# Query times key-value state in linear attention: one 64-row matmul per head, numerator and normaliser side by side, in place of block-diagonal 128-row ones

## The chip, the cores and the metric

The kernel runs on one core of a Trainium2 chip. A core has a matrix engine (PE, with its weight loads shown as PEld), a vector engine (DVE), a scalar engine (ACT), a general-purpose engine (POOL, also called GpSimd) and a queue engine (SP) that here only starts transfers. PE writes its results to PSUM, eight banks of 128 partitions by 512 four-byte values; the other data lie in SBUF. The metric is the device time of one execution in microseconds (us), as the median over runs.

## The reference

Two layers, each a modulated layer norm followed by a mixer, then another followed by a feed-forward part, with residual additions. Only the first mixer, linear attention with 32 heads of 64, is touched by the change; x is 4 x 512 x 512.

```python
q = relu(proj(Wq)); k = relu(proj(Wk)); v = proj(Wv)          # [b, 32, 512, 64]
kv = einsum('bhsd,bhse->bhde', k, v)                          # the state, 64 x 64 a head
qkv = einsum('bhsd,bhde->bhse', q, kv)
key_sum = k.sum(axis=2)
normalizer = clip(einsum('bhsd,bhd->bhs', q, key_sum), 1e-06, None)[..., None]
out = qkv / normalizer
return out.transpose(0, 2, 1, 3).reshape(b, s, INNER) @ Wo + bo
```

The second feed-forward part keeps the two largest of each four hidden values (stage D below); the first one routes rows to two of eight experts (stage B).

## The kernel before, in words

All matmuls of note are done with 32-bit operands split into a high and a low part (HI, LO): a product is three matmuls, HI by HI, HI by LO, LO by HI, accumulated in one bank. The helper `mm3` issues the three; its lines are L670 to L672, so most matmuls of the kernel stand under these lines and are told apart by their tile names. The split of a result takes two engines: ACT copies the HI part out of PSUM, then DVE subtracts it from the full value to get the LO part.

There is one program for each engine, written by hand in order; nothing schedules them but semaphores. Stage A (attention) has 8 groups of 4 heads (g), and in each a step for each of the 4 batch entries (b): 32 steps, s = 4g + b. The groups 1 to 6 are one loop body. Later stages are B (experts), C and D (sparse feed-forward).

One step on PE: four key/value projections of 128 rows each (t = 0 to 3, 12 matmuls of 512 columns, into bank 0 or 1), after each of which but the first the state of the tile before is accumulated in bank 4 (`accumulate(t-1)`, 6 matmuls of 130 columns, tiles kt and vt); two query projections, with the last accumulation between them; the output projection of the step before (`tail_a`, "tail" below, 24 matmuls with ot and the weights wo in W1b); and last the product of queries and state (12 matmuls, tiles kvb and qt). The four heads of a group form two pairs; a pair fills the 128 partitions of qt. The stationary tile kvb holds for each pair a block-diagonal 128x128 matrix of the two states (kind 0) and one of the two key sums, each repeated 64 times (kind 1), with zeros elsewhere, set once at the start. Kind 1 goes first, into banks 5 and 4, kind 0 after it into banks 6 and 7.

What happens to the result: DVE clips both normalisers from PSUM into rr (L1725), inverts pair 0 at the end of the step (`invert`, L1653) and pair 1 in the next step behind the low parts of tile 0. In the next step, at t = 2 and 3, `normalise` (L1658) multiplies the numerator in PSUM by rr; then `out_hi` on ACT (L1131) and `out_lo` on DVE (L1663) split it into ot, which the tail reads. The low parts of keys and values are L1673 and L1675, those of queries L1702, those of the state L1713 and L1715, and the evacuation of the tail is L1647. PE's `accumulate(0)` waits for both clips of the step before (r_max).

POOL adds the tail's results to x (L1978) and makes the low parts of weights that ACT has copied from a stage buffer (L1048 on ACT, `wsplit`, L1916 on POOL, 1024 columns each). In groups 1 to 6 the steps b = 1 and 2 split expert weights (tile W) and b = 3 splits two slices of the next attention weights (W1a), all ahead of the output's HI part in ACT's order; one further slice of these weights (W1b) is split at the end of b = 3 and one at the end of b = 0.

## Time and profile before

| | before |
|---|---|
| time, median of 3 runs | 2059.91 us (2056.55 to 2063.98) |
| profiled execution | 2059.06 us, span 2057.1 us |
| PE busy | 1835.3 us (89%), 8300 matmuls |
| weight loads busy | 1461.9 us (71%) |
| DVE busy | 1271.7 us (62%), 2094 instructions |
| ACT busy | 548.8 us (27%) |
| POOL busy | 775.0 us (38%) |

The busy time of PE is the sum of modelled spans that overlap, so it says that PE is hardly ever without a matmul, not that it runs at its peak. Stage A runs from about 25 to 1010 us.

### The profile page before, as it was taken

Reading aid. Unit: us, or ns where it says so; the run is one execution under the profiler, and the core shown is the slowest. Engines: PE = TensorE matmul, PEld = TensorE weight load, DVE = VectorE, ACT = ScalarE, POOL = GpSimd, SP = SyncE. Lnnn points to the kernel's source line nnn. Section 1 sums busy time; section 2 is a strip of 40 time slices with the busy share of each in tenths; the row PEclk is TensorE's granted clock in tenths of the full one; section 3 lists DMA queues with packets and bytes.
Section 4 is the critical chain, followed back from the end, with each engine's and each line's share of the span. In section 5 each row is a group of like instructions: output and inputs, shape, how many; then the busy total and the mean of one; then the engine's idle time right before and its main releaser. Section 6 shows DMA issues by size and latency. Waiting matters only on the chain.

```text
span 2057.1 us, 25161 instructions
## 1 busy us (share of the span) xinstructions
PE 1835.3 (89%) x8300; PEld 1461.9 (71%) x8300; DVE 1271.7 (62%) x2094; ACT 548.8 (27%) x1120; POOL 775.0 (38%) x565
## 2 busy tenths in 40 slices
PE   8999999999999999998547999735689999999996
PEld 5657888888888888877445777324478778787785
DVE  5665666666666666677852323588957565657574
ACT  2322222223222222212113343323342222212221
POOL 1545433433333333221350000475744454536342
PEclk9999999999999999999758999967799999999998
DMA  6211444434243525200146764330200111001011
GB/s 225 98 67 64 144 164 143 163 126 161 80 179 112 194 74 206 87 21 16 62 179 225 293 245 159 121 109 16 62 26 10 48 29 49 10 25 51 6 52 41
DMA packets 75070, 213.01 MB, mean 104 GB/s; under 512 B 6588, under 2 KB 6604, under 8 KB 72432
## 3 DMA queue, kind: packets, MB, share of 16 engines
q1 hardware_dynamic: 57072, 149.00, 20.5%
q0 software_dynamic: 6592, 42.04, 5.6%
q10 hardware_dynamic: 11328, 20.98, 3.4%
q8 instruction: 44, 0.72, 0.1%
q14 instruction: 34, 0.28, 0.0%
HBM read 126.20 MB, written 85.79 MB: 103 GB/s over the span
## 4 chain that ended last, share of the span: by engine, by line
PE 60%; DVE 21%; issue 9%; DMA 4%; POOL 3%; ACT 2%; DVEq 0%; ACTq 0%; POOLq 0%; SPq 0%
PE bank L670 19%; PE bank L672 18%; PE bank L671 18%; DMA hs_d<-yt 3%; DVE hh L1896 2%; PE bank L736 2%; DVE rr L1653 1%; POOL W1a L1916 1%; DVE st L1400 1%; POOL x L1978 1%; DVE tmp L1647 1%; DVE fl L1874 1%; DVE rstd L1384 1%; PE bank L701 1%; DVE xw L1452 1%
## 5 line engine op out<-in xcount | busy, mean ns | idle before, releaser
L1978 POOL TENSOR_TENSOR x<-x,tmp 128x512 f32<-128x512 f32 x192 | 264.8, 1389 | 484.3 <-DVE tmp L1647 431.3
L670 PE MATMUL bank<-hT,W1b 128*128 128x512 f32 x512 | 208.3, 407 | 11.4 <-DVE hh L1851 11.2
L1653 DVE RECIPROCAL rr<-rr 128x512 f32<-128x512 f32 x64 | 213.8, 3342 | 0.0
L670 PE MATMUL bank<-W1a,hT 128*128 128x512 f32 x512 | 206.9, 404 | 3.4 <-DVE hT L1579 3.4
L672 PE MATMUL bank<-W1a,hT 128*128 128x512 f32 x512 | 202.7, 396 | 0.0
L672 PE MATMUL bank<-hT,W1b 128*128 128x512 f32 x512 | 202.2, 395 | 0.0
L671 PE MATMUL bank<-hT,W1b 128*128 128x512 f32 x512 | 202.1, 395 | 0.0
L671 PE MATMUL bank<-W1a,hT 128*128 128x512 f32 x512 | 202.0, 394 | 0.0
L1144 ACT ACTIVATE kt<-bank 128x256 fp32r<-128x256 f32 x128 | 49.1, 384 | 551.4 <-PE bank L672 551.4
L1647 DVE TENSOR_TENSOR tmp<-bank,row 128x512 f32<-128x512 f32 x176 | 121.2, 689 | 78.3 <-PE bank L672 53.9
L1851 DVE TENSOR_TENSOR hh<-hh,bank 128x512 f32<-128x512 f32 x64 | 43.3, 687 | 184.9 <-PE bank L672 156.8
L1673 DVE SCALAR_TENSOR_TENSOR kt<-bank,kt 128x256 fp32r<-128x256 f32 x128 | 52.2, 408 | 147.4 <-ACT vt L1145 147.1
L1916 POOL TENSOR_TENSOR W<-stage,W 128x1024 fp32r<-128x1024 f32 x32 | 76.7, 2397 | 165.3 <-ACT W L1048 163.0
L670 PEld LDWEIGHTS bank<-hT,W1b 128*128 128x128 f32 x512 | 97.5, 190 | 35.5 <-DVE hh L1851 16.2
L670 PE MATMUL bank<-W1b,ot 128*128 128x512 f32 x256 | 105.8, 413 | 17.7 <-DVE tmp L1644 12.7
L670 PEld LDWEIGHTS bank<-W1a,hT 128*128 128x128 f32 x512 | 97.7, 191 | 27.7 <-issue 4.7
L672 PEld LDWEIGHTS bank<-hT,W1b 128*128 128x128 f32 x512 | 97.5, 190 | 22.2
L672 PEld LDWEIGHTS bank<-W1a,hT 128*128 128x128 f32 x512 | 97.4, 190 | 22.0
L670 PE MATMUL bank<-W,ad 128*128 128x512 f32 x256 | 101.6, 397 | 10.9 <-DVE ad L1903 9.1
L671 PEld LDWEIGHTS bank<-W1a,hT 128*128 128x128 f32 x512 | 97.8, 191 | 18.8
L671 PEld LDWEIGHTS bank<-hT,W1b 128*128 128x128 f32 x512 | 97.9, 191 | 18.5
L1345 ACT ACTIVATE ad<-hh 128x512 fp32r<-128x512 f32 x64 | 40.3, 632 | 252.7 <-DVE hh L1896 252.7
(258 smaller groups left out, 4424.0 us busy)
## 6 DMA issues: line engine op xcount, KB each, us to landing
hs_d<-bor SPq DMA_DIRECT2D x24, 1536.0 KB, 9.1
WB<-ws_d POOLq DMA_DIRECT2D x8, 3072.0 KB
ws_d<-W SPq DMA_DIRECT2D x18, 1024.0 KB, 6.4
stage<-wa SPq DMA_DIRECT2D x32, 512.0 KB, 5.1
row<-mod_rows_d ACTq DMA_DIRECT2D x52, 256.0 KB, 3.3
stage<-wbe SPq DMA_DIRECT2D x24, 512.0 KB, 3.9
stage<-wdn SPq DMA_DIRECT2D x24, 512.0 KB, 3.9
mw<-wmod SPq DMA_DIRECT2D x10, 1024.0 KB, 4.9
```

The costliest lines, as they stand in the source:

```text
L670: pe.matmul(o, lhs(HI), rhs(HI), start=start, stop=False, **kw)
L671: pe.matmul(o, lhs(HI), rhs(LO), start=False, stop=False, **kw)
L672: return pe.matmul(o, lhs(LO), rhs(HI), start=False, stop=stop, **kw)
L736: last = pe.matmul(o[0:NB, :], scT[:, layer, c, :], w[:, c * H:(c + 1) * H], start=c == 0, stop=c == NC - 1)
L1144: act.activation(kt[:, t % 2, HI, :], bank[t % 2][:, 0:256], ACT.Relu)
L1647: dve.tensor_tensor(tmp[:, par, :], TAIL[par][:, :], row[:, tb % 2, :], ALU.mult) \
L1653: dve.reciprocal(rr[:, pair, :], rr[:, pair, :]).then_inc(r_rec, 1)
L1673: dve.scalar_tensor_tensor(out=kt[:, t % 2, LO, :], in0=bank[t % 2][:, 0:256], scalar=0.0, in1=kt[:, t % 2, HI, :].bitcast(F32), op0=ALU.m ...
L1851: dve.tensor_tensor(hh[:, r, :], hh[:, r, :], bank[4 + r % 2][:, :], ALU.mult).then_inc(d_h, 1)
L1896: op(dve.scalar_tensor_tensor(out=hh[:, r, :], in0=flag, scalar=bound, in1=hh[:, r, :], op0=cmp, op1=ALU.mult))
L1916: return pool.tensor_tensor(dst, src, hi.bitcast(F32), ALU.subtract)
L1978: pool.tensor_tensor(xt, xt, tmp[:, (key + t) % 2, :], ALU.add).then_inc(ring_done, 1)
```

## The change

Each head gets a 64-row matmul of its own. Pair by pair, kvb now holds for partitions 0 to 63 the state of head 0 in columns 0 to 63 and its repeated key sum in columns 64 to 127; for partitions 64 to 127 it is the other way round. So there are no zeros in it, and it has half the size. A matmul with partitions 0 to 63 of kvb and qt writes numerators to the upper 64 partitions and normalisers to the lower 64 of one bank ("top"), one with partitions 64 to 127 the reverse in another ("low"): banks 5 and 6 for pair 0, 7 and 4 for pair 1. The matmuls of the two heads alternate. The count per step stays at 12.

The two numerators of a pair then lie in two banks. ACT gathers them in the new SBUF tile num (`num_out`, two copies of 64 partitions per pair), which shares its memory with the LO half of ot. The clip is written as two instructions of 64 partitions per pair, each shifting the normalisers to the other partition half. `normalise`, `out_hi` and `out_lo` work on num instead of PSUM. nn_full now counts two per step instead of four, and the new semaphore n_out counts ACT's copies; PE's first accumulation waits for it.

```diff
@@ -304,8 +304,12 @@
             return (a("kt", [P, 2, 2, 256], F32R), a("vt", [P, 2, 2, 2, VW], F32R), a("qt", [P, 2, 2, S], F32R),
-                    a("ot", [P, 2, 2, S], F32R), a("kvb", [P, 2, 2, 2, P], F32R), a("rr", [P, 2, S]),
+                    a("ot", [P, 2, 2, S], F32R), a("kvb", [P, 2, 2, P], F32R), a("rr", [P, 2, S]),
                     a("bor", [P, H]), a("colrow", [NB, H]))
+
+        def over_ot(a):
+
+            return a("before_num", [P, 5136]), a("num", [P, 2, S])
@@ -318,8 +322,8 @@
-        ((_, wm), (kt, vt, qt, ot, kvb, rr, bor, colrow), h2, (M_, crow, sqj, ct, cs),
-         (hh, mx, fl, ad)) = shared([over_pro, over_a, over_front, over_c, over_d])
+        ((_, wm), (kt, vt, qt, ot, kvb, rr, bor, colrow), (_, num), h2, (M_, crow, sqj, ct, cs),
+         (hh, mx, fl, ad)) = shared([over_pro, over_a, over_ot, over_front, over_c, over_d])
         hold3 = sb("hold3", [P, 9232])
@@ -373,6 +377,7 @@
         TAIL = bank[2:4]
+        NN = [(5, 6), (7, 4)]
         YB = [0, 1, 4, 5, 6, 7]
@@ -810,6 +816,7 @@
                         pe.wait_ge(r_max, s * 2)
+                        pe.wait_ge(n_out, s * 2)
                     for pair in range(2):
@@ -852,10 +859,13 @@
                 pe.wait_ge(kvb_lo, s + 1)
-                for kind, banks in ((1, (5, 4)), (0, (6, 7))):
-                    for pair in range(2):
-                        mm3(bank[banks[pair]][:, :], lambda h: kvb[:, h, pair, kind, :],
-                            lambda h: qt[:, h, pair, :], True, True).then_inc(nn_full, 1)
+                for pair in range(2):
+                    for i, (wl, wr) in enumerate(((HI, HI), (HI, LO), (LO, HI))):
+                        for head in range(2):
+                            q = slice(head * HD, (head + 1) * HD)
+                            last = pe.matmul(bank[NN[pair][head]][:, :], kvb[q, wl, pair, :], qt[q, wr, pair, :],
+                                             start=i == 0, stop=i == 2)
+                    last.then_inc(nn_full, 1)
@@ -931,8 +941,8 @@
                 pe.wait_ge(r_max, 2 * NB * GA)
+                pe.wait_ge(n_out, 2 * NB * GA)
                 pe.wait_ge(pj_lo, 6 * NB * GA)
-                pe.wait_ge(o_lo, 2 * NB * GA)
                 rows_transpose(0)
@@ -1128,7 +1138,14 @@
                 act.wait_ge(o_num, s * 2 + (pair - 1))
-                act.activation(ot[:, HI, pair, :], bank[6 + pair][:, :], ACT.Copy).then_inc(o_hi, 1)
+                act.activation(ot[:, HI, pair, :], num[:, pair, :], ACT.Copy).then_inc(o_hi, 1)
+
+            def num_out(s, pair):
+
+                act.wait_ge(nn_full, s * 2 + (pair + 1))
+                top, low = (bank[i] for i in NN[pair])
+                act.activation(num[0:HD, pair, :], top[0:HD, :], ACT.Copy)
+                act.activation(num[HD:P, pair, :], low[HD:P, :], ACT.Copy).then_inc(n_out, 1)
@@ -1172,7 +1189,7 @@
                     if pair == 0 and not (first and b == 0):
-                        act.wait_ge(nn_full, s * 4)
+                        act.wait_ge(nn_full, s * 2)
                     act.activation(qt[:, HI, pair, :], bank[pair][:, :], ACT.Relu).then_inc(pj_hi, 1)
@@ -1183,9 +1200,9 @@
                 for lo in (0, HD):
-                    q = slice(lo, lo + HD)
-                    act.activation(kvb[q, HI, :, 0, q], kv[q, :, q], ACT.Copy)
-                    ins = act.activation(kvb[q, HI, :, 1, q], kv[q, :, P:P + 1].to_broadcast([HD, 2, HD]), ACT.Copy)
+                    q, other = slice(lo, lo + HD), slice(HD - lo, P - lo)
+                    act.activation(kvb[q, HI, :, q], kv[q, :, q], ACT.Copy)
+                    ins = act.activation(kvb[q, HI, :, other], kv[q, :, P:P + 1].to_broadcast([HD, 2, HD]), ACT.Copy)
                 ins.then_inc(kvb_hi, 1)
@@ -1194,6 +1211,8 @@
                     split_a(g, 3)
+                for pair in range(2):
+                    num_out(s, pair)
@@ -1558,7 +1577,6 @@
                 dve.memset(bor[:, :], 0.0).then_inc(zero_ready, 1)
-                dve.memset(kvb[:, :, :, :, :].bitcast(F32), 0.0)
                 dve.memset(vt[:, :, HI, :, P:VW].bitcast(F32), 1.0)
@@ -1653,15 +1671,14 @@
             def normalise(s, pair):
-                dve.wait_ge(nn_full, s * 4 + (pair - 1))
+                dve.wait_ge(n_out, s * 2 + (pair - 1))
                 dve.wait_ge(r_rec, s * 2 + (pair - 1))
-                dve.tensor_tensor(bank[6 + pair][:, :], bank[6 + pair][:, :], rr[:, pair, :], ALU.mult) \
-                    .then_inc(o_num, 1)
+                dve.tensor_tensor(num[:, pair, :], num[:, pair, :], rr[:, pair, :], ALU.mult).then_inc(o_num, 1)
...
                 dve.wait_ge(o_hi, s * 2 + (pair - 1))
-                dve.tensor_tensor(ot[:, LO, pair, :], bank[6 + pair][:, :],
-                                  ot[:, HI, pair, :].bitcast(F32), ALU.subtract).then_inc(o_lo, 1)
+                dve.tensor_tensor(ot[:, LO, pair, :], num[:, pair, :], ot[:, HI, pair, :].bitcast(F32),
+                                  ALU.subtract).then_inc(o_lo, 1)
@@ -1709,21 +1726,21 @@
                 for lo in (0, HD):
-                    q = slice(lo, lo + HD)
-                    dve.tensor_tensor(kvb[q, LO, :, 0, q], kv[q, :, q], kvb[q, HI, :, 0, q].bitcast(F32),
-                                      ALU.subtract)
-                    last = dve.tensor_tensor(kvb[q, LO, :, 1, q], kv[q, :, P:P + 1].to_broadcast([HD, 2, HD]),
-                                             kvb[q, HI, :, 1, q].bitcast(F32), ALU.subtract)
+                    q, other = slice(lo, lo + HD), slice(HD - lo, P - lo)
+                    dve.tensor_tensor(kvb[q, LO, :, q], kv[q, :, q], kvb[q, HI, :, q].bitcast(F32), ALU.subtract)
+                    last = dve.tensor_tensor(kvb[q, LO, :, other], kv[q, :, P:P + 1].to_broadcast([HD, 2, HD]),
+                                             kvb[q, HI, :, other].bitcast(F32), ALU.subtract)
                 last.then_inc(kvb_lo, 1)
...
                 for pair in range(2):
-                    dve.wait_ge(nn_full, s * 4 + (pair + 1))
+                    dve.wait_ge(nn_full, s * 2 + (pair + 1))
                     if tail_of("A", g, b):
                         dve.wait_ge(o_num, s * 2)
-                    dve.tensor_scalar(rr[:, pair, :], bank[(5, 4)[pair]][:, :], 1e-6, None, ALU.max) \
-                        .then_inc(r_max, 1)
+                    top, low = (bank[i] for i in NN[pair])
+                    dve.tensor_scalar(rr[0:HD, pair, :], top[HD:P, :], 1e-6, None, ALU.max)
+                    dve.tensor_scalar(rr[HD:P, pair, :], low[0:HD, :], 1e-6, None, ALU.max).then_inc(r_max, 1)
                 invert(s + 1, 0)
```

On PE the place is the end of a step in the first group, the last matmuls of the tail (W1b, ot) and the product (qt, kvb). Before:

```order
L670 MATMUL bank<-W1b,ot 128x512
L671 MATMUL bank<-W1b,ot 128x512
L672 MATMUL bank<-W1b,ot 128x512
L670 MATMUL bank<-qt,kvb 128x512 [waits a_kvb_lo,a_proj_lo]
L671 MATMUL bank<-qt,kvb 128x512
L672 MATMUL bank<-qt,kvb 128x512
L670 MATMUL bank<-qt,kvb 128x512
L671 MATMUL bank<-qt,kvb 128x512
```

After:

```order
L676 MATMUL bank<-W1b,ot 128x512
L677 MATMUL bank<-W1b,ot 128x512
L678 MATMUL bank<-W1b,ot 128x512
L866 MATMUL bank<-qt,kvb 128x512 [waits a_kvb_lo,a_proj_lo]
L866 MATMUL bank<-qt,kvb 128x512 x11
L676 MATMUL bank<-W1a,hT 128x512 [waits a_proj_lo,ring_done]
L677 MATMUL bank<-W1a,hT 128x512
```

There are still twelve matmuls, now all under one line (L866), between the same neighbours; what moved is which rows and banks they use, and the waits ahead of them are the same.

On DVE the first place is the end of a step in the loop body, from the last evacuation of the tail (tmp) through the clips (rr) to the next step's first low parts (kt, vt). Before:

```order
L1647 TENSOR_TENSOR tmp<-bank,row 128x512 [waits ring_done,ring_full]
L1722 REGISTER_ALU
L1725 TENSOR_SCALAR rr<-bank 128x512 [waits a_out_normalised,a_norm_num_full]
L1722 REGISTER_ALU
L1725 TENSOR_SCALAR rr<-bank 128x512 [waits a_out_normalised,a_norm_num_full]
L1652 ISA
L1653 RECIPROCAL rr<-rr 128x512 [waits a_norm_clipped]
L1672 ISA
L1673 SCALAR_TENSOR_TENSOR kt<-bank,kt 128x256 [waits a_proj_hi]
L1675 TENSOR_TENSOR vt<-bank,vt 128x2x128
L1653 RECIPROCAL rr<-rr 128x512 [waits a_norm_clipped]
```

After:

```order
L1665 TENSOR_TENSOR tmp<-bank,row 128x512 [waits ring_done,ring_full]
L1738 REGISTER_ALU
L1742 TENSOR_SCALAR rr<-bank 64x512 [waits a_out_normalised,a_norm_num_full]
L1743 TENSOR_SCALAR rr<-bank 64x512
L1738 REGISTER_ALU
L1742 TENSOR_SCALAR rr<-bank 64x512 [waits a_out_normalised,a_norm_num_full]
L1743 TENSOR_SCALAR rr<-bank 64x512
L1670 ISA
L1671 RECIPROCAL rr<-rr 128x512 [waits a_norm_clipped]
L1689 ISA
L1690 SCALAR_TENSOR_TENSOR kt<-bank,kt 128x256 [waits a_proj_hi]
L1692 TENSOR_TENSOR vt<-bank,vt 128x2x128
```

Two clips have become four, of 64 partitions each, ahead of the same reciprocal.

The second place on DVE is the middle of the step: normalising, the low parts of the output and those of the queries (the last t in the loop body). Before:

```order
L1658 TENSOR_TENSOR bank<-bank,rr 128x512 [waits a_norm_inverted,a_norm_num_full]
L1672 REGISTER_ALU
L1673 SCALAR_TENSOR_TENSOR kt<-bank,kt 128x256 [waits a_proj_hi]
L1675 TENSOR_TENSOR vt<-bank,vt 128x2x128
L1658 TENSOR_TENSOR bank<-bank,rr 128x512 [waits a_norm_inverted,a_norm_num_full]
L1663 TENSOR_TENSOR ot<-bank,ot 128x512 [waits a_out_hi] x2
L1701 REGISTER_ALU
L1702 SCALAR_TENSOR_TENSOR qt<-bank,qt 128x512 [waits a_proj_hi]
L1701 REGISTER_ALU
L1702 SCALAR_TENSOR_TENSOR qt<-bank,qt 128x512 [waits a_proj_hi]
```

After:

```order
L1676 TENSOR_TENSOR num<-num,rr 128x512 [waits a_norm_inverted,a_num_copied]
L1689 REGISTER_ALU
L1690 SCALAR_TENSOR_TENSOR kt<-bank,kt 128x256 [waits a_proj_hi]
L1692 TENSOR_TENSOR vt<-bank,vt 128x2x128
L1676 TENSOR_TENSOR num<-num,rr 128x512 [waits a_norm_inverted,a_num_copied]
L1680 TENSOR_TENSOR ot<-num,ot 128x512 [waits a_out_hi] x2
L1718 REGISTER_ALU
L1719 SCALAR_TENSOR_TENSOR qt<-bank,qt 128x512 [waits a_proj_hi]
L1718 REGISTER_ALU
L1719 SCALAR_TENSOR_TENSOR qt<-bank,qt 128x512 [waits a_proj_hi]
```

Number and order are the same; the operand bank has become num in the three instructions of normalising and of the output's low part.

## Rows read from the trace of the kernel before

**Rows 1.** Windows: length, busy us of PE, PEld, DVE, ACT, POOL, clock, DMA, GB/s.
```profile
274.00:388.00 114.00, 113.68 (x545) 94.13 (x544) 74.00 (x108) 30.50 (x74) 39.56 (x24) 1.00 0.39 138
```

**Rows 2.** Timeline of PE, one step: start us, us, engine, line, operation.
```profile
486.26 0.39 PE L670 MATMUL bank<-qt,kvb 128*128 128x512 f32 x1
...
489.02 0.39 PE L670 MATMUL bank<-W1a,hT 128*128 128x512 f32 x1
...
494.48 0.22 PE L670 MATMUL bank<-vt,kt 128*128 128x130 f32 x1
...
497.92 0.22 PE L670 MATMUL bank<-vt,kt 128*128 128x130 f32 x1
...
508.23 0.40 PE L670 MATMUL bank<-W1b,ot 128*128 128x512 f32 x1
...
513.83 0.39 PE L670 MATMUL bank<-qt,kvb 128*128 128x512 f32 x1
```

**Rows 3.** Timeline of DVE, the same step.
```profile
487.15 1.38 DVE L1725 TENSOR_SCALAR rr<-bank 128x512 f32<-128x512 f32 x2
488.45 3.34 DVE L1653 RECIPROCAL rr<-rr 128x512 f32<-128x512 f32 x1
492.73 0.42 DVE L1673 SCALAR_TENSOR_TENSOR kt<-bank,kt 128x256 fp32r<-128x256 f32 x1 [0.94 <-ACT vt L1145]
...
496.94 0.41 DVE L1675 TENSOR_TENSOR vt<-bank,vt 128x256 fp32r<-128x256 f32 x1
...
503.00 0.69 DVE L1658 TENSOR_TENSOR bank<-bank,rr 128x512 f32<-128x512 f32 x1
504.70 1.29 DVE L1663 TENSOR_TENSOR ot<-bank,ot 128x512 fp32r<-128x512 f32 x2 [1.01 <-ACT ot L1131]
```

**Rows 4.** Timeline of PE, group 0, where 4-row transposes begin.
```profile
149.36 0.39 PE L672 MATMUL bank<-W1a,hT 128*128 128x512 f32 x1
149.68 0.41 PE L743 MATMUL bank<-ident,colrow 4*128 4x4 f32 x4
```

**Rows 5.** Groups by line and shape, attention stage: xcount, busy us, mean ns.
```profile
L1713 DVE TENSOR_TENSOR kvb<-bank,kvb 64x128 fp32r<-64x128 f32 x46 | 13.0, 284 | 0.3
```

**Rows 6.** Timeline of DVE and PE after the next product (T = 513.83).
```profile
517.36 1.28 DVE L1725 TENSOR_SCALAR rr<-bank 128x512 f32<-128x512 f32 x2
518.55 3.34 DVE L1653 RECIPROCAL rr<-rr 128x512 f32<-128x512 f32 x1
...
522.64 0.32 PE L670 MATMUL bank<-vt,kt 128*128 128x130 f32 x1 [0.43 <-DVE vt L1675]
```

**Rows 7.** Line L1663 (ns min/median/max), then timeline, stages D and C.
```profile
L1663 DVE TENSOR_TENSOR ot<-bank,ot x64: 669/682/692, 82.5 to 1009.0; 128x512 fp32r<-128x512 f32 x64
...
1606.05 2.41 POOL L1916 TENSOR_TENSOR W1b<-stage,W1b 128x1024 fp32r<-128x1024 f32 x1 [2.10 <-ACT W1b L1048]
1606.11 2.89 DVE L1870 TENSOR_TENSOR mx<-xn 128x512 f32<-128x512 f32 x1
...
1422.67 6.36 DVE L1452 TENSOR_TENSOR xw<-xw,crow 128x512 f32<-128x512 f32 x4
```

**Rows 8.** Timeline of POOL in the step of rows 2; line L1916, 209 to 850.
```profile
503.40 4.95 POOL L1916 TENSOR_TENSOR W1a<-stage,W1a 128x1024 fp32r<-128x1024 f32 x2 [14.87 <-ACT W1a L1048]
...
L1916 POOL TENSOR_TENSOR W<-stage,W x24: 2392/2408/2412, 226.0 to 811.7; 128x1024 fp32r<-128x1024 f32 x24
L1916 POOL TENSOR_TENSOR W1a<-stage,W1a x12: 2400/2404/2408, 281.3 to 839.3; 128x1024 fp32r<-128x1024 f32 x12
```

**Rows 9.** Groups by line and shape of ACT, attention stage.
```profile
L1131 ACT ACTIVATE ot<-bank 128x512 fp32r<-128x512 f32 x46 | 25.6, 603 | 4.7 <-DVE bank L1658 4.7
```

**Rows 10.** Timeline of PE in group 7 and after; windows view around the first.
```profile
916.35 0.48 PE L670 MATMUL bank<-vt,kt 128*128 128x130 f32 x1 [3.24 <-DVE vt L1675]
912.00:919.00 7.00, 3.76 (x14) 3.01 (x14) 5.72 (x29) 0.66 (x2) 0.00 (x0) 0.79 0.00 0
...
1009.69 0.80 PE L670 MATMUL bank<-W1b,ot 128*128 128x512 f32 x1 [4.95 <-DVE ot L1663]
```

More of the change, by code:

```diff
@@ L420, in build @@
         nn_full = sem("a_norm_num_full")
+        n_out = sem("a_num_copied")
         r_max = sem("a_norm_clipped")
@@ L1433, in apply_rows @@
                 if b >= 2:
-                    dve.wait_ge(nn_full, 4 * NB * GA)
+                    dve.wait_ge(nn_full, 2 * NB * GA)
                 for t in range(NT):
```

## Prediction

> **What bounds the kernel now.** The page comes first: PE is the busiest engine over the whole span. The windows view says where: in 114 us of attention in steady state PE is busy for 113.68, the vector engine DVE for 74.00 [rows 1]. A shorter PE stage looks like pure gain, so the question is what ends next when it is shorter. For that I followed one step of the attention stage in the timeline, engine by engine. T is the start of its first query-times-state matmul; in [rows 2] T = 486.26. The twelve matmuls take 489.02 - 486.26 = 2.76 us (0.23 each, start to start; a row says 0.39 because recorded spans overlap). Two key/value projections follow, then the first accumulation at T+8.22, a third projection, the second accumulation at T+11.66, then the output projection ("tail") at T+21.97, and the next product at T+27.57.
>
> DVE in the same step [rows 3]: it clips two normalisers from T+0.89, runs a reciprocal of 3.34, takes the low parts of tile 0's keys and values from T+6.47 after 0.94 idle for ACT, runs the second reciprocal, and has the low part of tile 1's values at T+10.68+0.41 = T+11.09. The second accumulation needs that, at T+11.66. So this chain has 0.57 us of slack against PE, and 0.94 of idleness inside. That is what a faster product meets, not the 40 idle microseconds of DVE in rows 1.
>
> **The product on PE.** It stays at 12 matmuls a step in 32 steps, each 512 columns, now with 64 rows. Nothing in this trace has 64 rows. Lower bound: two heads' matmuls, in separate row halves and banks, run side by side: 6 x 0.23 = 1.39. Upper bound: one after another, 2.76. A change of the rows in use costs too: ahead of the 4-row transposes the gap between starts is 0.32 instead of 0.23 [rows 4], 0.09 more. Leaving such a shape isn't shown alone; for entering and leaving I take 0.35, between 0.18 (0.09 twice) and 0.78 (two whole matmul records of 0.39). I take side by side, 1.39 + 0.35 = 1.74: 1.0 us saved a step, 32 us in all if PE alone decided. One after another it would lose 0.35 a step, 11 us. No row decides between them.
> The Trainium skill (TensorE: Matmul & The Clock Gate, Part 3: Packing small matmuls — row/col tiling) says that matmuls in different row groups overlap; by that rule the product takes the side-by-side time. The Trainium skill (TensorEngine Tiling (Array Packing), Key Properties) also says that a change of tiling mode drains the engine; the wider gap in rows 4 agrees.
>
> **The clipping on DVE.** One 128x512 instruction per pair becomes two of 64x512, because each head's bank holds the normaliser in its other half. Does half the height cost half? The 64x128 subtraction takes 0.28 [rows 5], a 128x256 one 0.41 and a 128x512 one 0.69 [rows 3]: these lie on one line in the elements of a row, 0.14 plus 0.27 for each 256, whatever the height. So each half costs a full one; at 1.19 for two, start to start [rows 6], a step gets +1.2. (If height counted, 0: the other bound.) The first can start when pair 0 is done, about T+1.1 (0.69 of matmuls, 0.2 for the switch, 0.2 to finish). The new chain: four clips to T+3.5, reciprocal to 6.75, keys and values to 7.4 (ACT has them an estimated 1.0 earlier than before, so nothing is waited for), reciprocal to 10.7, tile 1's values at T+11.3. The second accumulation starts at T+11.45, where PE could have been by T+10.6. Of the 1.0 saved, 0.2 is left in an ordinary step.
>
> **Late steps.** After the product of the fourth batch entry (T = 513.83) output additions on POOL hold up the last evacuations, and DVE clips only from T+3.53; PE already waits 0.43 for values [rows 6]. Here +1.2 goes straight to the end, and PE's saving does not help. I take 1.2 in group 0 and 0.6 in each of groups 1 to 6, since POOL's last split ends sooner relative to T once the step before is longer (next part): 4.8 us.
>
> **Normalising and the output's low part, now in SBUF.** These four DVE instructions a step keep number and size, but both inputs lie in SBUF; before, one was in PSUM. With one PSUM input 64 low parts took 0.669 to 0.692, none longer [rows 7], although POOL splits weights right beside them: two splits, 4.95 us from T+17.14 [rows 8], the low parts from T+18.44 [rows 3]. Now instructions with two SBUF inputs: in the sparse stage one began at 1606.11, beside a split from 1606.05 to 1608.46, and took 2.89 to 1609.00: it waited for the split's end. Four in a row beside POOL's work took 6.36, 1.59 each: the engines take turns [rows 7]. Put into the step: POOL's first split runs 17.2 to 19.6, once the second normalising is over. The first low part is asked for at 18.25, waits, runs 19.6 to 20.2. POOL's second split goes 20.25 to 22.65. The second low part runs 22.65 to 23.25, and the tail starts at T+23.31 in place of T+21.97: +1.34 a step. (Bounds: with no wait at all -0.2; behind both splits about the same 1.3.) Such pairs of splits stand in 18 steps of groups 1 to 6: 24 + 12 instructions [rows 8], two a step. 18 x 1.34 = 24.1 us, and one such step in group 0, 1.2.
> The Trainium skill (SBUF — State Buffer, Who interferes with whom) has this as a rule: a DVE instruction with two SBUF inputs and a GpSimd one that reads SBUF exclude each other, and the first to issue wins. It speaks against this change, and the trace agrees (2.89 for 0.69).
>
> **The rest.** ACT gets four copies of 64x512 a step, 0.6 each by its 128x512 copy [rows 9], done by about T+3.5; PE asks for them at the first accumulation, T+7. ACT is idle until the first projection ends. That cover of 3.5 us is what hides them; without it they would cost what they lack. In group 0 three steps leave DVE time, and PE's saving shows in two: -2. In group 7 one step gains 0.2; the one where PE waits 3.24 for DVE gets +1.2; two later ones an estimated 0.6 each; after the last step PE waits 4.95 for the output's low part, +1.2 [rows 10]. Together +3.4. The clearing of kvb that goes away stands before the first input has arrived: 0. Outside attention nothing changes.
>
> **Sum.** 24.1 + 1.2 + 4.8 + 3.4 - 2 = +31.5. The profiled execution took 2059.06 (span 2057.10, 1.96 around it), 0.85 below the median of 2059.91. 2059.06 + 31.5 = 2090.6; I say 2090.
>
> **Rivals.**
> 1. *Serial halves.* For it: no 64-row matmul in the trace, so nothing shows that two run at once. The product then takes 3.1; pair 1 is clipped only from T+3.1, the chain ends at T+12.2, 0.85 later than in my case, in about 24 steps: +20, 2110.
> 2. *No turn-taking at the low part.* DVE gets both its turns after the first split and is done at T+20.9, before the tail's need. Against it: 1.59 each for four in a row [rows 7]. Then 31.5 less 19 x 1.4 is +5: 2064.
> 3. *PE's saving shows (faster).* The place is the clip: if 64 rows cost about half of 128, the chain ends at T+10.2 and PE is the bound at both accumulations. It decides only if the low parts also slip past the splits; then 32 x 1.0 less: 2027, and 2043 with half of it. Against it: rows 5 with rows 3.
> 4. *The clock.* Around the 3.24 wait the granted clock averages 0.79 over 7 us [rows 10]: 2.9 us at the lower level (1.2 GHz), some 1.5 us lost. If a wait of 1.3 before each tail did this too, 19 x 1.5 = 28 more: 2118. Against it: the 0.43 wait stands in a stage at 1.00 [rows 1, 6]; no row here has one of 1.3.
>
> **Numbers.** Forecast 0.50 (2080 to 2100), serial 0.20, no turns 0.13, faster 0.09, clock 0.08. Less than 0.3% (6 us) can't be told from no change in this kernel. Faster than that 0.08, within it 0.10, slower 0.82. Range 2064 to 2114: it takes in serial and most of no turns, and leaves out the clock and the gain.
>
> **What would show it.** Right: 1.7 us from the first 64-row matmul to the next projection; 64x512 clips of 0.69; low parts of up to 2.9 us in 18 steps and PE idle before the tail there; PE waiting for tile 1's values in most steps. Wrong: low parts at 0.69 throughout; 64-row matmuls 0.23 apart one by one; clips at 0.4; no wait at the second accumulation.

## The result, and the profile after

| | before | changed |
|---|---|---|
| time, median of 4 runs each | 2061.94 us (2056.55 to 2064.02) | 2097.03 us (2095.99 to 2099.69) |
| profiled execution | 2059.06, span 2057.1 | 2096.59, span 2094.6 |
| product of the fourth entry of the last group starts | 998.26 | 1029.01 |

The changed kernel is slower, by a ratio of 1.0176 (interval 1.0152 to 1.0200), about 35 us. The last row of the table shows that 31 of them have come by the end of attention's steps (T of the last product). I use that moment below wherever a run can be compared by attention alone; the later stages are the same code and move by a few us from run to run. A *late step* is one that begins with the product of the fourth batch entry; the *ordinary steps* are the other 18 of groups 1 to 6.

The page of the profile after, the engines' busy time and the chain that ended last:

```profile
PE 1821.1 (87%) x8300; PEld 1421.6 (68%) x8300; DVE 1374.1 (66%) x2157; ACT 626.5 (30%) x1248; POOL 782.0 (37%) x565
...
PE 49%; DVE 26%; issue 12%; DMA 4%; ACT 4%; POOL 4%; ACTq 0%; DVEq 0%; POOLq 0%; SPq 0%
```

PE has less to do and the time is longer: its busy time fell by 14 us, DVE's rose by 102. About four steps by windows, from the same groups as [rows 1] (the columns are those of [rows 1]):

```profile
284.00:401.00 117.00, 109.79 (x527) 86.53 (x526) 87.62 (x112) 38.95 (x88) 40.21 (x25) 0.99 0.38 134
```

PE stands idle for 7.2 us of the 117 where it stood idle for 0.3 of 114. An ordinary step, beginning with the product at T = 703.26, shows both places. PE (timeline: start, busy, line, tiles, and in brackets the idle time ahead and what ended it):

```profile
702.93 0.40 PE L678 MATMUL bank<-W1b,ot 128*128 128x512 f32 x1
703.26 1.66 PE L866 MATMUL bank<-qt,kvb 64*128 64x512 f32 x12
704.85 0.50 PE L676 MATMUL bank<-W1a,hT 128*128 128x512 f32 x1
705.18 0.40 PE L677 MATMUL bank<-W1a,hT 128*128 128x512 f32 x1
...
711.31 0.30 PE L676 MATMUL bank<-vt,kt 128*128 128x130 f32 x1 [0.71 <-DVE vt L1692]
...
714.99 0.33 PE L676 MATMUL bank<-vt,kt 128*128 128x130 f32 x1
...
726.60 0.50 PE L676 MATMUL bank<-W1b,ot 128*128 128x512 f32 x1 [1.03 <-DVE ot L1680]
```

The product takes 1.59 us from its first matmul to the next projection, where [rows 2] show 2.76. At each change of rows two starts are 0.33 behind their neighbour and not 0.23. One of the two lies outside the product at either end (702.93 to 703.26, 704.85 to 705.18), so the net gain is 2.76 - 1.59 - 0.2 = 0.97 us. It is then waited away: 0.71 at the first accumulation, for the low part of the values, and 1.03 ahead of the tail, for the output's low part. The tail now starts at T+23.34 (T+21.97 before, [rows 2]). The same step on DVE:

```profile
704.27 0.69 DVE L1742 TENSOR_SCALAR rr<-bank 64x512 f32<-64x512 f32 x1 [0.21 <-PE bank L866]
704.97 0.68 DVE L1743 TENSOR_SCALAR rr<-bank 64x512 f32<-64x512 f32 x1
705.69 0.69 DVE L1742 TENSOR_SCALAR rr<-bank 64x512 f32<-64x512 f32 x1
706.39 0.68 DVE L1743 TENSOR_SCALAR rr<-bank 64x512 f32<-64x512 f32 x1
707.11 3.35 DVE L1671 RECIPROCAL rr<-rr 128x512 f32<-128x512 f32 x1
710.38 0.36 DVE L1690 SCALAR_TENSOR_TENSOR kt<-bank,kt 128x256 fp32r<-128x256 f32 x1
710.66 0.41 DVE L1692 TENSOR_TENSOR vt<-bank,vt 128x256 fp32r<-128x256 f32 x1
...
720.17 0.68 DVE L1676 TENSOR_TENSOR num<-num,rr 128x512 f32<-128x512 f32 x1
721.91 4.56 DVE L1680 TENSOR_TENSOR ot<-num,ot 128x512 fp32r<-128x512 f32 x2 [1.06 <-ACT ot L1141]
```

DVE goes from the first clip to the values without a gap; before, it had 0.94 to spare there [rows 3]. And the two low parts, 1.29 for both in [rows 3], take 4.56. What runs beside them is POOL's pair of splits, 4.95 before [rows 8]:

```profile
720.49 5.43 POOL L1933 TENSOR_TENSOR W<-stage,W 128x1024 fp32r<-128x1024 f32 x2 [15.06 <-ACT W L1058]
```

Over all 64 low parts (view of one line's instructions: minimum, median, maximum in ns), and how long PE waited for them (us, times):

```profile
L1680 DVE TENSOR_TENSOR ot<-num,ot x64: 670/1750/2892, 82.0 to 1041.3; 128x512 fp32r<-128x512 f32 x64
...
  PE bank L676: 26.8, 19
```

From product to product an ordinary step takes 29.11 to 29.23 us, 27.55 to 27.57 before: +1.6 on the mean, 28.7 in all 18.

### The profile page after: what moved, and what is told of

Its sections match the earlier page's. It is cut to its first block, busy times and chain, and to the rows that moved or that the text cites. A ratio compares the mean times of both kernels' runs of the same rounds, so it can differ in the third digit from the quotient of the medians.

```text
span 2094.6 us, 25406 instructions
## 1 busy us (share of the span) xinstructions
PE 1821.1 (87%) x8300; PEld 1421.6 (68%) x8300; DVE 1374.1 (66%) x2157; ACT 626.5 (30%) x1248; POOL 782.0 (37%) x565
## 4 chain that ended last, share of the span: by engine, by line
PE 49%; DVE 26%; issue 12%; DMA 4%; ACT 4%; POOL 4%; ACTq 0%; DVEq 0%; POOLq 0%; SPq 0%
PE bank L676 15%; PE bank L678 14%; PE bank L677 14%; DMA hs_d<-yt 3%; DVE rr L1671 3%; DVE hh L1913 2%; DVE ot L1680 2%; PE bank L742 2%; DVE rr L1743 2%; POOL W1a L1933 1%; DVE st L1419 1%; ACT W L1058 1%; PE bank L866 1%; DVE tmp L1665 1%; POOL x L1995 1%
## 5 line engine op out<-in xcount | busy, mean ns | idle before, releaser
L1933 POOL TENSOR_TENSOR W<-stage,W 128x1024 fp32r<-128x1024 f32 x32 | 82.5, 2577 | 168.6 <-ACT W L1058 166.3
L676 PEld LDWEIGHTS bank<-W1a,hT 128*128 128x128 f32 x512 | 97.7, 191 | 37.3 <-issue 13.8
L1680 DVE TENSOR_TENSOR ot<-num,ot 128x512 fp32r<-128x512 f32 x64 | 104.3, 1657 | 21.2 <-ACT ot L1141 20.1
L678 PEld LDWEIGHTS bank<-W1a,hT 128*128 128x128 f32 x512 | 97.5, 190 | 22.1
```

Of the source, the lines that this page charges most:

```text
L676: pe.matmul(o, lhs(HI), rhs(HI), start=start, stop=False, **kw)
L678: return pe.matmul(o, lhs(LO), rhs(HI), start=False, stop=stop, **kw)
L1680: dve.tensor_tensor(ot[:, LO, pair, :], num[:, pair, :], ot[:, HI, pair, :].bitcast(F32), ALU.subtract).then_inc(o_lo, 1)
L1933: return pool.tensor_tensor(dst, src, hi.bitcast(F32), ALU.subtract)
```

## The experiments

All were run on one chip per set, with the kernel before at 2060 to 2061 us in each set; ratios are to it. "Last product" is the moment of the table above. Cut lines of a diff are marked "...".

### 1. Both splits behind the low parts

In steps b = 1 to 3 POOL waits until the output's low parts are made, and splits then.

```diff
-                if b == 3 and not (isinstance(g, int) and g == GA - 1):
+                last = isinstance(g, int) and g == GA - 1
+                if b > 0 and not (last or (first and b < 3)):
+                    pool.wait_ge(o_lo, (g * NB + b) * 2)
+                if b == 3 and not last:
                     for j in range(2 if first else 3):
                         split_a(g + 1, j)
...
```

> The changed kernel, and POOL waits for the output's low parts before its weight splits (steps b = 1 to 3). Turn-taking theory (a low part with two SBUF inputs waits for a split on POOL): low parts go back to 0.67 us each, the 1.0 us wait of PE before the output projection goes, step of 29.1 becomes 27.9; 18 x 1.2 = 22 us less, but the later splits can push POOL's additions and the clips of the step after b = 3, up to 6 back: 2075 to 2081. Rival (PE waits there for ACT or for a slower SBUF read, whatever POOL does): low parts stay long, 2097.

Measured: 2114.03 us (2110.12 to 2116.51), ratio 1.0263 (1.0246 to 1.0280). The low parts are back to 1.29 for both, there is no wait ahead of the tail, and the ordinary steps take 27.80 to 27.85: 1.3 less, as the turn-taking explanation says. But the six late steps of groups 1 to 6 go from 28.7 to 30.2 up to 34.2 to 35.8. I had looked at the place where the wait helps, not at what follows it on POOL (timeline of POOL around one product at T = 291.39):

```profile
283.74 4.95 POOL L1933 TENSOR_TENSOR W1a<-stage,W1a 128x1024 fp32r<-128x1024 f32 x2 [17.89 <-DVE ot L1680]
291.92 2.40 POOL L1933 TENSOR_TENSOR W1b<-stage,W1b 128x1024 fp32r<-128x1024 f32 x1 [3.22 <-ACT W1b L1058]
294.27 5.01 POOL L1995 TENSOR_TENSOR x<-x,tmp 128x512 f32<-128x512 f32 x4
```

The third split and the additions come late, the evacuations wait for the additions, the clips wait for the evacuations, and start at T+6.25 (T+2.00 in the changed kernel). PE then waits 5.5 to 6.1 us for values in each of the six, and the clock falls: its mean over the step of T = 646.79 is 0.86. The upper end of the forecast, 2081, was missed by 33 us.

### 2. Reciprocals behind the low parts of keys and values

Both reciprocals are taken out of the way of the tiles that PE waits for: pair 0 after tile 0's low parts, pair 1 after tile 1's.

```diff
-                        if t == 0:
-                            invert(s, 1)
+                        if t < 2:
+                            invert(s, t)
...
-                invert(s + 1, 0)
```

> The changed kernel with each of the two reciprocals one tile later (pair 0 behind tile 0's low parts, pair 1 behind tile 1's), all else the same. Theory (the chain clip, clip, clip, clip, reciprocal, low parts, reciprocal, low parts is what ate PE's gain): both accumulations wait no more, the second starts at 10.6 instead of 11.7 us after the product; about 1.1 less in 19 steps and 1.5 to 2 less in 7 late ones: 2097 - 21 - 12 = 2064. The 1.0 wait before the output projection stays. Rival (PE's gain is eaten by something else, such as waiting for ACT's evacuation): less than 8 us gained.

Measured: 2064.61 us (2058.75 to 2069.85), ratio 1.0020 (1.0008 to 1.0031), last product 996.99. Nothing but DVE's order is changed, and 32 us come back. In groups 1 to 6 the first accumulation starts at T+7.16 and the second at T+10.60, neither with a wait; ordinary steps take 27.9 to 28.0, late ones 26.6. The wait of 1.01 ahead of the tail stays, with low parts of 4.55 for both. In group 0 two steps became longer (41.56 and 48.84, from 37.95 and 44.49): in the first of them PE now waits 2.97 for values at the third accumulation. In the late steps of groups 1 to 6 the clips still start as late as T+2.2 and the step has no wait: late clips cost their time there through the order of DVE, and by themselves cost nothing.

### 3. The kernel before with four clips

```diff
-                    dve.tensor_scalar(rr[:, pair, :], bank[(5, 4)[pair]][:, :], 1e-6, None, ALU.max)
+                    dve.tensor_scalar(rr[0:HD, pair, :], o[0:HD, :], 1e-6, None, ALU.max)
+                    dve.tensor_scalar(rr[HD:P, pair, :], o[HD:P, :], 1e-6, None, ALU.max)
```

> The kernel before with only the clips changed: each of the two 128x512 clips a step written as two of 64x512 in the same bank. Theory (half the height costs a full instruction, 0.7 each here, +1.5 a step, hidden by slack in ordinary steps and open in late ones): clips at 0.69, ordinary steps unchanged within 0.1 (27.6), late ones +1.4 in 7 steps, after the last step +1.5, group 7 up to +1.5: +10 to +14, 2073. Rival (64 rows cost half): clips at 0.4, 2062.

Measured: 2084.01 us (2082.98 to 2087.18), ratio 1.0116 (1.0099 to 1.0133), last product 1017.19, 18.9 later. The clips of one step (timeline of DVE):

```profile
266.08 0.68 DVE L1726 TENSOR_SCALAR rr<-bank 64x512 f32<-64x512 f32 x1
266.78 0.69 DVE L1727 TENSOR_SCALAR rr<-bank 64x512 f32<-64x512 f32 x1
267.50 0.68 DVE L1726 TENSOR_SCALAR rr<-bank 64x512 f32<-64x512 f32 x1
268.20 0.69 DVE L1727 TENSOR_SCALAR rr<-bank 64x512 f32<-64x512 f32 x1
```

Half the height costs the full 0.69, and they start 0.70 to 0.72 apart, where two clips of 128 rows were 0.60 apart ([rows 6]). Here this splits within one bank and shifts nothing across the halves, and costs the same as in the changed kernel, so neither the shift nor the second bank is the reason. The ordinary steps hide nearly all of it (27.8, +0.24); the late ones of groups 1 to 6 do not (30.3 to 31.6, +1.8 to +3.3). The clips were forecast rightly, but the time missed the forecast of +10 to +14 by 10 us: a late step had been given only 1.4. In two of the six, and in the late step of group 0, the clock fell behind the wait (mean 0.94 over the step of T = 406.92, which takes 31.32, and 1.00 over that of T = 292.99, which takes 30.55).

### 4. The kernel before with the numerator in SBUF

The block-diagonal product stays; ACT copies the numerators to num, and normalising and the output's parts read them there.

```diff
...
+                act.activation(num[:, pair, :], bank[6 + pair][:, :], ACT.Copy).then_inc(n_out, 1)
...
-                dve.tensor_tensor(ot[:, LO, pair, :], bank[6 + pair][:, :],
+                dve.tensor_tensor(ot[:, LO, pair, :], num[:, pair, :],
```

> The kernel before with its block-diagonal product and its banks, but ACT copies the two numerators (128x512 each) to num in SBUF, and normalising and the output's parts work there. Turn-taking theory: low parts of up to 2.9 us beside POOL's splits, PE waits 1.2 before the output projection in 18 steps, 18 x 1.4 = 25, less 3 for late steps: 2084. Rival (it is the 64-row product or its waits that costs, not SBUF inputs): 2062.

Measured: 2079.74 us (2077.17 to 2081.23), ratio 1.0095 (1.0078 to 1.0112), last product 1013.38, 15.1 later. The low parts take what they take in the changed kernel:

```profile
254.41 4.57 DVE L1673 TENSOR_TENSOR ot<-num,ot 128x512 fp32r<-128x512 f32 x2 [1.05 <-ACT ot L1136]
```

Ordinary steps 28.84 to 28.94 (+1.3), late ones 27.55 to 27.6 (-0.9, since POOL's third split then ends sooner relative to T). Experiments 3 and 4 move the last product by 18.9 and 15.1, 34.0 us in sum, and the whole change moves it by 30.8. If the two simply add, which no run shows, the side-by-side product gives back only some 3 us of its 32 x 0.97.

### 5. The three matmuls of a head in a row

```diff
-                    for i, (wl, wr) in enumerate(((HI, HI), (HI, LO), (LO, HI))):
-                        for head in range(2):
+                    for head in range(2):
+                        for i, (wl, wr) in enumerate(((HI, HI), (HI, LO), (LO, HI))):
```

> The changed kernel with only the order of the twelve 64-row matmuls altered: for each pair all three of head 0, then all three of head 1. If two neighbours run side by side only when they stand in different row halves (my theory: the matmuls are issued in order, and 1.59 us for twelve comes from the alternation), three of four neighbours share a half and follow each other 0.23 apart: the product takes 2.3 to 2.8 us in place of 1.59, the clips of pair 0 start about 0.4 later, the first and second accumulation are late by that, and the time is 2097 + 32 x 0.4 = 2110 (2104 to 2118). Rival: the halves have queues of their own and the order doesn't matter: product 1.59, time 2097.

Measured: 2097.85 us (2096.26 to 2099.10), ratio 1.0181 (1.0149 to 1.0214); product 1.59 or 1.60. My expectation was wrong and its rival right: alternating the halves one by one is not needed, runs of three overlap as well. PE, same place as above:

```profile
705.13 1.67 PE L866 MATMUL bank<-qt,kvb 64*128 64x512 f32 x12
706.72 0.50 PE L676 MATMUL bank<-W1a,hT 128*128 128x512 f32 x1
```

### 6. All twelve matmuls in one half

That left open whether two halves work at once or a 64-row matmul is simply cheaper. Here head 0 is computed twice and head 1 not at all:

```diff
-                            q = slice(head * HD, (head + 1) * HD)
+                            q = slice(0, HD)
```

> The changed kernel in which all twelve 64-row matmuls of a product use partitions 0 to 63 (head 0 is computed twice, head 1 not at all), so that no two of them can run side by side. Theory (two halves at once): they follow each other 0.23 apart, the product takes 2.8, the clips of pair 1 start at about T+1.6 and T+3.0, the four clips end at T+4.4 in place of 3.85 and PE has 0.6 to 1.2 less to wait: +0.3 to +1.0 a step, the last product about 10 to 30 us later than 1029. Rival (a 64-row matmul of 512 columns costs half of a 128-row one by itself): product 1.59, nothing changes. The values that follow differ, so the experts' stage may take another number of slots: the place of the last product and the product's length decide.

Measured: product 2.94 us, last product 1048.49 (19.5 later than in the changed kernel), 2133.54 us in all.

```profile
715.68 3.01 PE L866 MATMUL bank<-qt,kvb 64*128 64x512 f32 x12
718.62 0.50 PE L676 MATMUL bank<-W1a,hT 128*128 128x512 f32 x1
```

A 64-row matmul costs a full 0.23 from start to start (2.94 for twelve, with two changes of rows in it); the gain is that two halves work at once. The Trainium skill (TensorE: Matmul & The Clock Gate, Why this matters for your kernels) says both: a matmul of few rows takes as long as a full one, and the gain lies in running distinct row groups concurrently. The traces agree, with 2.94 for one half and 1.59 for two.

### 7. One turn for DVE between the two splits

Experiment 1 held both splits back. Here only the second waits, in the steps that split expert weights as shown and in those of b = 3 between the first two slices. In an ordinary step it starts at T+21.2 in place of T+20.0.

```diff
...
                     split_e(g, 2 * b - 2)
+                    pool.wait_ge(o_lo, (g * NB + b) * 2)
                     split_e(g, 2 * b - 1)
```

> The changed kernel with one wait on POOL: in the steps of b = 1, 2 and 3 the second of the two weight splits starts only when both low parts of the output are made, the first one stays where it is. Turn-taking theory: DVE gets both its turns after the first split (19.7 to 21.0 after T), the low parts are done 2.3 earlier, the tail starts at T+22.1 without a wait, and an ordinary step takes 27.9 in place of 29.13: 19 x -1.2 = -23; the second split starts only 0.7 later than now (20.9 in place of 20.2), unlike when both splits were held back, so the late steps gain at most 1 us each: +0 to +7. Time 2077 (2072 to 2084). Rival: any wait that binds POOL to DVE is passed on to POOL's additions and comes back in the late steps, as when both splits were held back: 2092 to 2110.

Measured: 2092.10 us (2088.54 to 2095.09), ratio 1.0154 (1.0118 to 1.0190), last product 1023.66. The low parts take 2.35 for both, no wait is left ahead of the tail (T+22.14), ordinary steps are 27.83: -1.3 each, as expected. But the late steps of groups 1 to 6 take 30.1 to 32.8. The number fits the rival; its mechanism does not. POOL's third split starts at T+25.57 of the step before, 25.40 in the changed kernel: the wait hardly delays it. What happened is that PE's step got 1.3 shorter and POOL's did not, so the clips start at T+3.45 (T+2.00 in the changed kernel) and PE waits 3.0 to 3.2 us for the values in each of the six. In four of them the clock then falls. Windows of the one at T = 295.47 (columns as above, the granted clock third from the end), and PE behind the wait:

```profile
302.00:304.00 2.00, 0.79 (x4) 0.33 (x2) 2.00 (x1) 0.66 (x2) 0.00 (x0) 1.00 0.00 0
304.00:306.00 2.00, 0.03 (x1) 0.06 (x1) 2.00 (x4) 0.00 (x0) 0.00 (x0) 0.77 0.00 0
306.00:308.00 2.00, 2.00 (x8) 1.90 (x9) 2.00 (x1) 0.00 (x0) 0.00 (x0) 0.50 0.00 0
308.00:310.00 2.00, 2.00 (x7) 1.52 (x6) 1.59 (x3) 0.00 (x0) 0.00 (x0) 0.50 0.00 0
310.00:312.00 2.00, 2.00 (x6) 1.58 (x5) 0.00 (x0) 0.00 (x0) 0.00 (x0) 0.53 0.00 0
312.00:314.00 2.00, 2.00 (x13) 1.77 (x12) 0.80 (x3) 0.66 (x2) 0.00 (x0) 1.00 0.00 0
```

```profile
305.97 0.45 PE L676 MATMUL bank<-vt,kt 128*128 128x130 f32 x1 [3.17 <-DVE vt L1692]
...
307.28 0.73 PE L676 MATMUL bank<-W1a,hT 128*128 128x512 f32 x1
...
312.24 0.22 PE L676 MATMUL bank<-vt,kt 128*128 128x130 f32 x1
```

Six accumulations take 1.31 us and twelve projections 4.96, 6.27 together, where an ordinary step has 3.68 from the first accumulation to the second. So the wait of 3.17 is followed by another 2.5 us lost at 1.2 GHz: this step of 32.76 is 27.83, 2.45 for the later first accumulation, and 2.5 for the clock. The two late steps whose clock stays at 1.00 take 30.12 and 30.27: 27.83 and 2.3 to 2.4, with nothing else.

### 8. The same, with POOL's additions ahead of the third split

The test of that reading: take the late clips away, leave all else.

```diff
-                    if not first:
-                        split_a(g + 1, 2)
...
                 if not first:
                     ln_out(ln, 1)
+                if b == 3 and not (first or last):
+                    split_a(g + 1, 2)
```

> The kernel with only the wait between POOL's two splits (2092), and the third split of b = 3 (W1b) moved behind POOL's additions; the reciprocals stay where the changed kernel has them. Theory: what held its late steps at 31.5 was one wait of 3.2 us, which the later clips caused, and the half clock that followed. With the additions first the clips start at T+1, the wait is 0.7 as in an ordinary step, the clock stays at 1.00 and a late step of groups 1 to 6 takes 27.85 in place of 31.5 to 32.8: -4 x 6 = -24, 2068 (2062 to 2073). Rival: the half clock comes from something else in the late step and stays: 2085 to 2092.

Measured: 2064.93 us (2059.42 to 2070.07), ratio 1.0022 (1.0009 to 1.0034), last product 1001.14. In the late steps of groups 1 to 6 the clips start at T+1.01, the wait is 0.56 to 0.77, the clock stays at 1.00, and the step takes 27.80 to 27.87. The late step of group 0, which the edit leaves alone, keeps a wait of 3.31 and half clock behind it (33.01). So the half clock came with the long waits and went with them.

### 9. One turn, and the reciprocals later in groups 1 to 7

The two causes removed together: the wait on POOL of experiment 7 and the order on DVE of experiment 2, this one in groups 1 to 7 only.

> The changed kernel with the wait between POOL's two splits and, in groups 1 to 7 only, both reciprocals moved behind the low parts of keys and values of tiles 0 and 1. Two-chain theory (late clips through the reciprocal and the values, 1.2 to 1.5 a step; turns at the output's low part, 1.0 to 1.3 a step; nothing else): ordinary steps 26.9, where PE has no wait left, late steps 26.6 to 28, group 0 as in the changed kernel: 2097 - 18 x 2.25 - 6 x 2 = 2045 (2036 to 2056), faster than the kernel before. Rival: with PE's steps that short POOL becomes the bound (its splits, additions and layer-norm parts take about as long), the late steps stay at 29 and ordinary ones at 27.5: 2062 to 2070.

Measured: 2039.40 us (2035.97 to 2043.12), ratio 0.9890 (0.9858 to 0.9923), last product 974.17. It is the first version faster than the kernel before. DVE in an ordinary step, now with the clips, the keys and the reciprocal in the new order, and the low parts between POOL's splits:

```profile
586.78 0.68 DVE L1745 TENSOR_SCALAR rr<-bank 64x512 f32<-64x512 f32 x1
589.06 0.42 DVE L1690 SCALAR_TENSOR_TENSOR kt<-bank,kt 128x256 fp32r<-128x256 f32 x1 [1.59 <-ACT vt L1162]
...
589.73 3.34 DVE L1671 RECIPROCAL rr<-rr 128x512 f32<-128x512 f32 x1
...
601.07 2.36 DVE L1680 TENSOR_TENSOR ot<-num,ot 128x512 fp32r<-128x512 f32 x2 [1.06 <-ACT ot L1141]
```

From 583.65 to 610.27, product to product, PE has no wait that the timeline shows: 26.62, 0.95 less than before the change. Late steps take 27.4 to 27.6, for there the clips still start at T+3.4 to T+3.6.

### 10. All of it, with the additions first

The edit of experiment 8 on top of experiment 9.

> The kernel with the wait between POOL's splits and the reciprocals behind the low parts (2039), in which POOL makes the third weight split of b = 3 (W1b) after its additions and not before. Theory: the last evacuations and the clips of the late steps start at T+1 in place of 3.4 and the step takes 26.6 in place of 27.5, in six steps: -5, 2034 (2029 to 2039). Rival: in these steps DVE's low parts come first anyway and the waits of 0.2 are all there is; or the split is then late for the tail: 2039 to 2045.

Measured: 2033.14 us (2027.74 to 2034.45), ratio 0.9850 (0.9832 to 0.9868), last product 966.94. Late steps take 26.60. This is the best version: 28 us faster than the kernel before, 64 faster than the changed one.

### 11. The reciprocals later in the kernel before

The control: is the gain only the order?

> The kernel before with the reciprocals moved in the same way in groups 1 to 7: the control for what that order of DVE is worth without the 64-row matmuls. Theory: in the ordinary steps before, PE is itself the bound at both accumulations (0 gained), and only the seven late steps have a wait for DVE: -0.4 to -1 each: 2056 (2052 to 2061). Rival: the ordinary steps gain too, as with the 64-row matmuls: 2040 or less.

Measured: 2058.57 us (2055.16 to 2063.67), ratio 0.9983 (0.9966 to 1.0000), last product 992.23. The gain of 2.6 is at the edge of what the runs can tell. Ordinary steps stay at 27.6 to 27.8, late ones fall from about 28.4 to 27.6. There PE is the bound, and DVE's order is worth 0.8 us in a late step alone. Since PE waits for nothing in these steps, the other two edits would have no wait to remove here (argued, not run), and the remaining 25 us of experiment 10 need the side-by-side product. The places where they come fit that: 24.1 lie in the 24 steps of groups 1 to 6, 1.0 a step, which is what one product saves.

### 12. Experiment 9 with all matmuls in one half

> The kernel with the wait between POOL's splits and the reciprocals behind the low parts (2039), again with all twelve matmuls in partitions 0 to 63 (head 1 not computed). There PE waits for nothing in the ordinary steps, so the product's length must come through whole: product 2.8, ordinary steps 26.63 + 1.2 = 27.85, and the last product of attention 974 + 32 x 1.2 = 1011 to 1014. Rival (half cost by itself): 974.

Measured: product 2.94, ordinary steps 27.95 to 27.99, last product 1009.40, 2094.03 us in all (head 1 not computed, so later stages are not compared). The last product lands just ahead of the forecast of 1011 to 1014. The ordinary step is 1.35 longer, the whole difference of the products: once DVE and POOL are out of the way, PE's saving shows in full.

## Why the prediction was right

The forecast was 2090 and the measured median 2097.03, slower as predicted; its likeliest case is the one that the traces show, both mechanisms included. That the size came so close is in part luck, as the sum shows. Step by step, in the order of its sum:

- **Product side by side.** 1.74 predicted with both changes of rows, 1.59 + 0.2 measured: the saving of 1.0 is 0.97, and experiment 9, with no wait left, has a step 0.95 shorter than before. The open question, serial halves, is settled by experiment 6, and that rival's price was good in total: it gave 20 more than the forecast, and one half costs 19.5 more than the changed kernel at the last product.
- **Clipping.** That each half costs a full clip was right; the term was mis-sized. I took the spacing of two full clips, 0.60 [rows 6], and it is 0.71, so a step gets 1.55 and not 1.2. The second accumulation starts at T+11.73, not T+11.45, and the 0.2 that was to be left in an ordinary step is gone.
- **Late steps.** 4.8 predicted, 5.8 measured. In groups 2 to 6 it is 0.57 a step (0.6 predicted) and in group 0 1.22 (1.2 predicted). The excess is group 1 alone, 1.76. There a wait of 1.73 was followed by half clock, which I had priced only for the waits ahead of the tail (windows of the changed kernel, step of T = 294.37):

```profile
304.00:306.00 2.00, 2.00 (x10) 1.62 (x10) 2.00 (x1) 0.00 (x0) 0.00 (x0) 0.77 0.00 0
306.00:308.00 2.00, 2.00 (x6) 1.59 (x5) 1.04 (x3) 0.00 (x0) 0.00 (x0) 0.50 0.00 0
```

- **Normalising and the low part in SBUF.** The turn-taking is there as put together: split, low part, split, low part. The tail starts 1.40 later on the mean (1.34 predicted). The 0.2 that an ordinary step costs beyond that come behind the tail's start: 5.79 from there to the product in place of 5.60, of which 0.1 is the change to 64 rows and 0.1 the first matmul after the wait (0.33 to the next one). So 18 steps give 28.7, not 24.1. This term was furthest off, by 4.6: 3.4 for what lies behind the tail's start, which it put at nothing, and 1.1 for the 0.06 ahead of it. The step of group 0 that was given 1.2 has the long low parts (4.56) but no wait, and lost nothing.
- **The rest.** ACT's copies are done by T+3.43 and nobody waits for them. Group 0 gained 3.1 (2 predicted), but 2.0 of it is the step after the second entry, 46.49 before and 44.49 after. Experiments 3 and 4, with the old product, have 44.79 there, at a mean clock of 1.00. The kernel before had a lower one over that step (the first row is before, the second after):

```profile
97.60:144.10 46.50, 42.97 (x181) 27.29 (x180) 27.07 (x54) 11.08 (x24) 18.99 (x20) 0.96 0.24 85
97.30:141.70 44.40, 40.23 (x181) 25.83 (x180) 28.40 (x56) 13.52 (x28) 18.86 (x20) 1.00 0.25 87
```

So 1.7 of the 3.1 is luck with the clock, and PE's saving there is 1.4. In group 7 the steps up to the last product, given +2.2, came to -0.4: the wait of 3.24 grew to 5.98, as the late clips would have it, yet that step is only 0.2 longer, with a mean clock of 0.89 in place of 0.85. After the last step the tail starts 1.57 later (1.2 predicted), with a wait of 7.60.
- **Sum.** 28.7 + 5.8 - 3.1 - 0.4 + 1.6 - 0.2 (the first product starts that much earlier) = 32.4 for attention, 31.5 predicted. Errors of 4.6, 1.0 and 0.4 upward and of some 5 downward nearly cancel, and that is luck; without the downward ones the sum would have been 37.5, still slower and within the range. The profiled executions differ by another 5 us in later stages, whose code is unchanged and which had been given 0: about 3 in the experts' stage, which I did not pursue, and about 2.4 where the sparse stage begins. There the granted clock was lower after the change (0.81 over 1530 to 1540, where the kernel before has 0.93 over 1495 to 1505). The medians differ by 35.1, so 3 rather than 5 of this stand in them.
- **Rivals.** *No turn-taking* is refuted by 4.56 for 1.29. *PE's saving shows* is refuted for this kernel by clips of 0.69, yet experiment 12 shows the saving in full where both waits are gone. *The clock* did not fall with the wait of 1.03 ahead of the tail, as argued (1.00 over 325 to 900, with fifteen such waits); it fell in a late step.

The prediction treated the two losses as given. It named POOL's splits and the order on DVE as causes, but not that both yield to small edits, two reciprocals moved and one wait added: this part was found by running it.

## What to carry to other kernels

- A faster step on PE pays only if the engines that feed it have slack at that place. Look at which wait ends last ahead of each use, and move the long instruction that nobody needs yet (here a reciprocal of 3.35) behind the short one that PE waits for: it brought back 32 of the 35 us that the change had cost.
- Before holding work back on an engine, follow its queue to the end. Holding both splits back cost 17 us, holding only the second one gained 5, and with the additions moved ahead 32.
- Two fixes that gain 5 and 32 us alone (experiments 7 and 2) gained 58 together: with experiment 7 alone PE still waits for values in every step, most of all in the late ones, and with experiment 2 alone ahead of the tail.

## What the runs showed of the hardware that was not expected

- The overlap of the two row halves does not depend on alternating single matmuls: 1.59 us with runs of one and with runs of three.
- The same wait in the same place of the step was followed by half clock in some groups and not in others: in experiment 7 after 3.17 (T = 295.47), but not after 3.17 two groups later (T = 527.92); in experiment 3 after 1.95 but not after 2.38; in the changed kernel after 1.73 but not after 2.00. So the length of the last wait alone does not tell, and the cost of one (0 to 2.5 us on top of itself) could not be told beforehand here. What else decides was not tried.
- POOL pays for the turns too, but little: 5.43 in place of 4.95 for its pair, while DVE pays 4.56 for 1.29.
- In group 0 the step after the second entry takes 44.5 us in the changed kernel and 47.4 to 47.7 in those of experiments 7 to 10, though nothing in it was edited. The clock tells them apart: its mean over the step is 1.00 in the changed kernel and 0.93 in all four. Why it fell there in one execution and not in another is open, so a difference of 2 to 3 us at this place says nothing about an edit.
